# Linear attention in 128-token chunks with its normalisation on GpSimd, and a recurrence of 98 steps on 512 columns

## The reference

```python
def _L1_attn_ref(x, W, b):                 # x is the layer-normed t
    qkv = (x @ W.T + b).reshape(Bx, Tx, 3, Dx)
    q, k, v = (qkv[:, :, 0], qkv[:, :, 1], qkv[:, :, 2])
    q = jax.nn.elu(q) + 1.0
    k = jax.nn.elu(k) + 1.0
    kv = jnp.einsum('bti,btj->btij', k, v)
    kv_cum = jnp.cumsum(kv, axis=1)
    k_cum = jnp.cumsum(k, axis=1)
    num = jnp.einsum('bti,btij->btj', q, kv_cum)
    den = jnp.einsum('bti,bti->bt', q, k_cum)[..., None] + 1e-06
    return num / den
def _L1_ffn_ref(x, W, V, gamma, beta):     # x is the layer-normed t
    Wx = jnp.einsum('bti,hi->bth', x, W)
    ...                                    # batch norm over all tokens, gamma, beta
    def step(yt, wx_t):
        yt = jax.nn.sigmoid(wx_t + yt @ Vt)
        return (yt, yt)
...
t = t + _L1_attn_ref(_ln_t(t), L1_attn_W, L1_attn_b)
t = t + _L1_ffn_ref(_ln_t(t), L1_ffn_W, L1_ffn_V, L1_ffn_gamma, L1_ffn_beta)
```

## Time and profile before

| quantity | value |
|---|---|
| median of 3 runs | 2030.25 us (2029.51 to 2030.74) |
| profiled execution | 2031.14 us, of which the span of instructions is 2029.5 us |
| PE busy over the span | 1923.1 us (95%) |
| DVE / ACT / POOL busy | 1677.6 (83%) / 1465.6 (72%) / 1290.2 us (64%) |
| mean granted TensorE clock | 0.98 |

### The profile page before, as it was taken

The page is one execution under the profiler, slowest core; times in us unless marked ns, Lnnn a source line. Parts: engine busy times, 40 slices in busy tenths (PEclk is TensorE's granted clock), DMA queues, the critical chain, the costliest instruction groups (busy, mean ns, idle before and its releaser), DMA issues. The chain is left out here.

```text
span 2029.5 us, 64530 instructions
## 1 busy us (share of the span) xinstructions
PE 1923.1 (95%) x20434; PEld 1672.5 (82%) x20434; DVE 1677.6 (83%) x5427; ACT 1465.6 (72%) x3774; POOL 1290.2 (64%) x1760
## 2 busy tenths in 40 slices
PE   4999999999999997999999999999999995699997
PEld 2888888888888886899999999999999993466664
DVE  7888888888888885799999999999999992355554
ACT  3777777777777775799999999999999981122221
POOL 3888888888888885444544444444444445577772
PEclk9999999999999999899999999999999996899998
DMA  4343434443434322122222222222222212366663
GB/s 137 106 110 106 109 108 110 106 112 104 113 103 111 94 78 73 38 62 62 59 61 61 59 62 60 59 63 59 59 63 59 59 51 63 109 199 199 187 210 110
DMA packets 228620, 190.53 MB, mean 94 GB/s; under 512 B 19264, under 2 KB 187552, under 8 KB 228448
## 3 DMA queue, kind: packets, MB, share of 16 engines
q1 hardware_dynamic: 228448, 188.22, 33.3%
HBM read 111.08 MB, written 77.07 MB: 93 GB/s over the span
## 5 line engine op out<-in xcount | busy, mean ns | idle before, releaser
L830 POOL TENSOR_SCALAR la_spread<-la_mv 112x4 f32<-112x4 f32 x231 | 54.6, 236 | 388.5 <-DVE la_mv L916 388.1
L536 POOL TENSOR_TENSOR wa_prob<-wa_prob,wa_peak 128x784 f32<-128x784 f32 x128 | 194.5, 1520 | 118.4 <-DVE wa_peak L425 118.4
L788 ACT ACTIVATE la_raised<-k_psum,la_bqk 128x224 f32<-128x224 f32 x448 | 200.6, 448 | 73.9 <-PE k_psum L682 73.9
L838 POOL TENSOR_TENSOR la_ln<-la_spread,k_exponent 112x4 f32<-112x4 f32 x231 | 239.5, 1037 | 1.8 <-ACT la_u L771 0.3
L1274 ACT ACTIVATE main_y<-k_psum,sc_cols 128x448 f32<-128x448 f32 x112 | 70.9, 633 | 209.1 <-PE k_psum L1215 209.1
L682 PE MATMUL k_psum<-la_uT,la_wt 128*128 128x224 f32 x896 | 211.2, 358 | 0.0
L771 ACT ACTIVATE la_u<-la_xc,la_ln 112x128 f32<-112x128 f32 x448 | 201.1, 515 | 13.3 <-POOL la_ln L842 13.2
L805 ACT ACTIVATE la_u<-la_tn,la_ln 112x128 f32<-112x128 f32 x448 | 201.0, 515 | 10.2 <-POOL la_ln L842 10.2
L543 POOL TENSOR_TENSOR wa_prob<-wa_prob,wa_inv 128x784 f32<-128x784 f32 x128 | 194.8, 1522 | 10.1 <-DVE wa_inv L389 10.1
L789 ACT ACTIVATE la_positive<-k_psum,la_bqk 128x224 f32<-128x224 f32 x448 | 200.8, 448 | 0.0
L417 DVE TENSOR_TENSOR wa_prob<-k_psum,wa_bias 128x784 f32<-128x784 f32 x128 | 124.9, 976 | 83.1 <-PE k_psum L272 83.1
(11 more groups left out here) (147 smaller groups left out, 5879.2 us busy)
## 6 DMA issues: line engine op xcount, KB each, us to landing
wa_xw<-in_x_tok SPq DMA_DIRECT2D x128, 224.0 KB, 2.7
wa_xT<-in_x_cm SPq DMA_DIRECT2D x128, 196.0 KB, 2.5
la_xc<-x SPq DMA_DIRECT2D x224, 112.0 KB, 2.0
t<-la_tn SPq DMA_DIRECT2D x224, 112.0 KB, 2.0
main_tb<-t SPq DMA_DIRECT2D x28, 896.0 KB, 6.0
out<-main_ob SPq DMA_DIRECT2D x28, 896.0 KB, 7.6
x<-wa_y SPq DMA_DIRECT2D x128, 112.0 KB
x<-wa_y SPq DMA_DIRECT2D x128, 56.0 KB
```

The costliest lines, as they stand in the source:

```text
L536: nc.gpsimd.tensor_tensor(s, s, peak[:, k % S, :].unsqueeze(2).broadcast_to([128, PAIRS * HEADS, WIN]), ALU.subtract).then_inc(lowered, 1)
L788: nc.scalar.activation(raised[:, k, j, :], src, ACT.Exp, bias=bqk[:, j:j + 1])
L838: nc.gpsimd.tensor_tensor(rstd, spread[:, :], exponent[0:CH, 0:4], ALU.pow).then_inc(rooted, 1)
```

## The change

- Linear attention takes chunks of 128 tokens across image borders, 196 units of 256 tokens. A chunk that an image border cuts in half (`splits`) is masked and takes its outer product from its second half alone.
- The bias, and the mean over the weights that makes it cover the subtraction, are folded into the weights once (`fold`). The features of q and k come from one exp over 512 columns (ACT, `exps`, L793) and one max/min on DVE that reads PSUM (`combine`, L898).
- The running state is summed in PSUM: `outer(n, 0)` and `outer(n, 1)` each add one product, ACT copies the state out after each (`keep_state`, L817). DVE loses `advance`, `carry` and `values_out`.
- Both normalisations move from ACT to POOL, where each is a pair of tensor_scalar instructions on 128x128 (`normalise(n+2)`, L849, and `normalise2(n-5)`, L860). They stand behind `statistics(n+3)` in POOL's list.
- Everything is written out, no hardware loop is left.
- `scan` runs 98 steps on 512 columns (32 segments an image), in 14 batches of SB = 7; its input needs one POOL pass; the warm call has 2 batches of 6. The scale table goes out to memory and back before it.

```diff
             @block.gpsimd
             def _(pool):
                 pool.wait_ge(prep, 1)
-                def statistics(n, k):
+                def statistics(n):
...
                     pool.wait_ge(aggregated, n + 1)
-                    at_least(pool, shifted, n)
-                    apart(pool, passed)
-                    moments = mv[:, k].rearrange("p l a m -> p (l a) m")
-                    nc.gpsimd.tensor_scalar(spread[:, :], moments[:, :, 1], LN_EPS, None, ALU.add).then_inc(spread_out, 1)
-                    nc.gpsimd.tensor_scalar(minus[:, :], moments[:, :, 0], -1.0, None, ALU.mult).then_inc(minus_out, 1)
...
+                    nc.gpsimd.tensor_scalar(spread[:, :], mv[:, n % S].rearrange("p l a m -> p (l a) m")[:, :, 1], LN_EPS, None,
+                                            ALU.add).then_inc(spread_out, 1)
+                    pool.wait_ge(spread_out, n + 1)
+                    nc.gpsimd.tensor_tensor(rstd[:, n % S, :], spread[:, :], exponent[:, 0:4], ALU.pow).then_inc(rooted, 1)
...
+                def normalise(n):
+                    pool.wait_ge(rooted, n + 1)
+                    for a in range(2):
+                        last = nc.gpsimd.tensor_scalar(u[:, n % S, a, :], xc[:, n % XS, a, :], mv[:, n % S, 0, a, 0:1],
+                                                       rstd[:, n % S, a:a + 1], ALU.subtract, ALU.mult)
+                    last.then_inc(normed, 1)
...
-                def step(n, k):
-                    remember(n - AHEAD, k % S)
-                    statistics(n + 3, (k + 3) % S)
-                pipeline(pool, step, **run)
+                for n in steps:
+                    statistics(n + 3)
+                    normalise(n + 2)
+                    normalise2(n - 5)
...
-                def step(n, k):
-                    queries_and_keys(n, k % S)
-                    turn_keys(n - 1, (k - 1) % S)
-                    turn_tokens(n + 1, (k + 1) % S)
-                    numerators(n - 3, (k - 3) % S)
-                    moments(n - 8, k % S)
-                    outer(n - 2, (k - 2) % S)
-                    values(n + 1, (k + 1) % S)
-                    scores(n, k % S)
-                pipeline(pe, step, **run)
+                for n in steps:
+                    queries_and_keys(n)
+                    turn_keys(n - 1)
+                    turn_tokens(n + 1)
+                    outer(n - 2, 0)
+                    numerators(n - 3)
+                    moments(n - 8)
+                    outer(n - 2, 1)
+                    values(n + 1)
+                    scores(n)
...
+                for n in steps:
+                    measure(n + 3)
+                    denominators(n - 3)
+                    combine(n)
+                    invert(n - 3)
+                    aggregate(n + 3)
+                    attend(n - 3)
+                    inner_out(n)
...
+                for n in steps:
+                    exps(n)
+                    keys_out(n - 1)
+                    turned_out(n + 1)
+                    keep_state(n - 2, 0)
+                    values_out(n + 1)
+                    keep_state(n - 2, 1)
...
-        scan(nc, t2, out, 0, fT, vT, shift_bn, rstd, shift, start, final, ident, bank, "main")
+        scan(nc, t2, out, 0, 7, fT, vT, shift_bn, rstd, start, final, ident, bank, "main")
```

More of the change, by code:

```diff
@@ L620, in linear_attention, with rows, begins, splits @@
         k_turned, k_out = sem("la_k_turned"), sem("la_k_out")
-        kv_ready, moved, advanced = sem("la_kv_ready"), sem("la_moved"), sem("la_advanced")
+        kv_ready, kept = sem("la_kv_ready"), sem("la_kept")
         num_ready, den_ready, den_inv, attended = sem("la_num_ready"), sem("la_den_ready"), sem("la_den_inv"), sem("la_attended")
         normed2, counted, gram_done = sem("la_normed2"), sem("la_counted"), sem("la_gram_done")
[L625 to L631, removed]
+        def rows(dram, n):
+            return dram.rearrange("b t c -> (b t) c")[n * 2 * P:(n + 1) * 2 * P, :].rearrange("(a p) c -> p a c", p=P)
+        def begins(c):
+            return (c * P) % T == 0
+        def splits(c):
+            return (c * P) // T != (c * P + P - 1) // T
+        def ends(c):
+            return ((c + 1) * P) % T == 0
+        def outers(c):
+            return sum(not ends(i) for i in range(c))
+        steps = range(-4, UNITS + 9)
         with nc.Block() as block:
@@ L650, in store @@
+                def store(n):
+                    if not inside(n, UNITS):
                         return
                     sp.wait_ge(attended, n + 1)
-                    sp.dma_start(chunks(t2, n), tn[:, k]).then_inc(stored[k], 16)
-                def step(n, k):
-                    load(n + 4, (k + 4) % XS)
-                    store(n - 4, (k - 4) % XS)
-                pipeline(sp, step, **run)
+                    sp.dma_start(rows(t2, n), tn[:, n % XS]).then_inc(stored[n % XS], 16)
@@ L720, in outer @@
                         return
[L721 to L729 removed]
+                    if a == 0:
+                        pe.wait_ge(k_out, n + 1)
+                        pe.wait_ge(v_out, n + 1)
@@ new lines, in aggregate @@
+                def aggregate(n):
+                    if not inside(n, ROWS):
+                        return
+                    dve.wait_ge(measured, n + 1)
+                    at_least(dve, normed, min(UNITS, n - S + 1))
+                    at_least(dve, normed2, n - S - AHEAD + 1)
+                    for which, m in ((0, n), (1, n - AHEAD)):
+                        if inside(m, UNITS):
+                            for a in range(2):
+                                last = nc.vector.bn_aggr(mv[:, n % S, which, a, :], stats[:, n % S, which, a, :])
+                    last.then_inc(aggregated, 1)
@@ L1156, in _ @@
             def _(sp):
-                def step(j, k):
+                for j in range(-3, NB + 2):
                     if inside(j + 3, NB):
-                        kl = 1 - k
                         if out is not None:
@@ L1276, in _ @@
-                pipeline(act, step, **run)
+                for t in range(NT):
+                    act.wait_ge(v_done, t + 1)
+                    if out is not None:
+                        at_least(act, y_turned, t - 1)
+                    nc.scalar.activation(y[:, t % 2, :], b_state[t % 2][:, 0:COLS], ACT.Sigmoid, bias=shift_bn).then_inc(y_made, 1)
         if repeated:
```

585 lines of the change are left out of this document (267 added, 318 removed).

## The result

The changed kernel takes 2327.98 us (median of 4 runs, 2327.46 to 2329.79) against 2030.11 us (2029.51 to 2030.74) of the kernel before on the same chip. The ratio is 1.1469, with a 95% interval of 1.1449 to 1.1489: 14.7% slower. The forecast was slower by 220 us, to 2250, with a range up to 2313. The loss is 298 us, and the time lies outside the range.

What follows compares the result with a forecast made beforehand. A loop through PE, DVE and POOL was to bound linear attention at 5.49 us a unit instead of PE's 3.99. 221 - 2 + 0 + 1 = +220 us gave 2250 us, range 2190 to 2313.

Steps and rivals of the forecast that it cites:

- The loop: Linear attention: a chain through PE, DVE and POOL sets a 5.49 us period, PE idling 1.4 us before L682.
- Point 6 of the loop: POOL's pair of tensor_scalar on 128x128 takes 0.72 us, 0.38 an instruction; bounds 0.45 and 1.33.
- Points 4 and 5: On the loop: DVE to POOL 0.22 us; POOL's epsilon, power and two waits on its own results 1.62 us.
- Points 1, 2, 3 and 7: On the loop: PE's work 1.42 us; to combine 0.40; combine to aggregate 0.69, aggregates 0.36; POOL to PE 0.06.
- POOL's pair is dear: Rival, 4 in 100: POOL's normalisation pair at its upper bound, or slowed by DVE reading SBUF; period 6.10, time 2369 us.
- The clock: Rival, 3 in 100: PE's idling drops its granted clock; between 2250 and 2742 us, some 2500 if half the time.
- PE's work of 3.99 us: Linear attention: PE's work after the change sums to 3.99 us for a unit of 256 tokens.
- nothing else in a step is late: Linear attention: combine ends in time before scores, ACT's work and state copies fit, POOL's own load is 3.2 us.
- Ends of the stage: Linear attention's start about 1.5 us longer, its end about as much shorter: zero, within 3.
- The recurrence: The scan calls: main steps -6.4 us, warm call +3.0, main start +2.1, last store +3.5, prologue -1; together +1, within -5 and +9.

Runs made afterwards that it cites:

- Experiment 1: Changed kernel with one line moved in POOL's list, normalise(n+2) ahead of statistics(n+3): 2066.94 us, ratio 1.0183 to the kernel before.
- experiment 7: Changed kernel with only u's normalisation back on ACT, POOL computing a shift for it: 1986.18 us, ratio 0.9792 to the kernel before.
- experiment 2: Changed kernel, same order, POOL's four tensor_scalar a unit using multiply and add instead of subtract and multiply (values differ): 2188.49 us, ratio 1.0780.
- experiment 4: Changed kernel with an extra stage ahead timing tensor_scalar forms on POOL, alone and beside DVE: 2369.18 us (one run).
- experiment 6: Experiment 5 with combine(n) ahead of denominators(n-3) in DVE's list: 1956.55 us, ratio 0.9639 to the kernel before.
- experiment 3: Changed kernel with both edits, normalise(n+2) ahead of statistics(n+3) and multiply-add on POOL (values differ): 1980.82 us, ratio 0.9757.
- experiment 5: Changed kernel with normalise(n+2) ahead of statistics(n+3), the normalisation adding a mean negated by one small POOL instruction: 1981.33 us, ratio 0.9766.

## Why the prediction was wrong

The mechanism, its place and its direction were right; a term of its sum was mis-sized, the pair of tensor_scalar on the loop, and with it the time fell outside the range.

- **The loop.** Right, and shown. PE idles before L682, released by L849, 1.59 us a unit (308.6 / 194; 1.4 forecast). Experiment 1 opens the loop by order alone and gives 261 us back; experiment 7 opens it by taking the pair off POOL and gives 342.
- **Point 6 of the loop, the failed step.** It put the pair of tensor_scalar at 0.72 us; it measured 1.58, above its upper bound of 1.33 too. That bound was two rows of a form that multiplies and adds, and the pair subtracts. The step took the row of the same instruction name and the nearest size without asking whether its two operations were the same. Experiments 2 and 4 show that the operation is the cause of 353 of the 421 ns that an instruction took over the forecast (801 - 448). The other 68 are an error of the line itself: a fixed part of 342 ns where it had 240, made up in part by 0.83 ns a column where it had 1.13.
- **Points 4 and 5, too dear.** The way from DVE to POOL was 0.09, not 0.22. L837 to L841 was 0.36, not 0.41. And `normalise` follows the power after 1.03 us, where 1.04 + 0.17 had been added: it waits for `rooted` of the unit before, so there was no wait on POOL's own last result. That could be read in the order of POOL's list, and the prediction even says that the normalisation needs only older statistics; its sum did not use it. Together -0.36 us in this unit.
- **Points 1, 2, 3 and 7.** The first two 1.59 together plus 0.19, forecast 1.62 and 0.20; `combine` to aggregate 0.67 (0.69); aggregate 0.36 (0.36). Right within 0.03 each. Pair and way to PE 1.64, forecast 0.78. The whole: 5.49 + 0.86 - 0.42 = 5.93, the unit shown; the mean is 5.88. Point 6's error alone is 0.86 x 195 = 168 us; errors that cancelled hid half of it, and that was luck.
- **The rival "POOL's pair is dear"**, 4 in 100, is what happened, 0.8 us an instruction, though its time of 2369 was too high, for it kept the dear points 4 and 5. Its other suggested cause, DVE's reading of SBUF, is excluded by experiments 2 and 4 as more than the 8 ns between 793 and 801. The chance was too small for an operation that no row showed.
- **The clock.** The rival is false: the granted clock was 1.00 over 1165 us with PE 73% busy and an idle of 1.6 us in each period. The rows were the right guide. The Trainium skill, TensorE: Matmul & The Clock Gate, § A second HAM failure mode, tells of another kernel, in bf16 with 512 columns, in which short idles between groups of matmuls made the clock swing. Carried over to this kernel, as the prediction's rival did, that does not agree with this trace.
- **PE's work of 3.99 us** is right: 3.994 in experiment 6. But "nothing else in a step is late" was wrong by 0.12 us: with the loop open, `scores` waits for `combine` (experiments 3 and 6). It costs nothing at a period of 5.88, and 24.8 us at 4.1 (1981.33 - 1956.55).
- **Ends of the stage.** Forecast zero within 3, measured +6.9. The first `values` start at 817.7 instead of 813.6 (+4.1). POOL's first statistics start 2.2 us later (811.8 instead of 809.6), behind DVE's folding of the weights, which ends at 810.9. From there to the first `values` it is 5.9 us instead of 4.0, with two statistics and a pair of 1.59 ahead of them; in experiment 6 it is 4.0 again (812.7 to 816.7). At the other end, from the last `values` to the first DMA of the recurrence, it is 22.9 us instead of 20.1 (+2.8). Experiment 1, which mends the order and keeps the subtraction, has 22.8 there, and experiment 2, which does the reverse, 18.9. So POOL's dear instructions lengthen the end, not the loop.
- **The recurrence.** Forecast +1 within -5 and +9, measured -8.6, outside these bounds (338.1 us from its first DMA to the end of the span, against 346.7). Main steps are 2.581 apart, not 2.603 (-8.5 instead of -6.4). The start of the main call was forecast 2.1 later; from its first load to its first sigmoid it was 0.4 shorter, the load landing after 7 us where 9 were taken. The warm call was even, not +3. The end was +1.1, not +3.5; the prologue -0.95, as forecast. All but the prologue erred to the dear side.

In sum: 298.3 + 4.1 + 2.8 - 8.6 = 296.6 us of span, from 2029.5 to 2326.1, against 221 - 2 + 0 + 1 forecast. The period is where the forecast failed: 298 us against 219.

## What to carry to other kernels

When work moves to another engine's list, follow the lists round once: an instruction placed behind a wait that it does not need can close a loop through several engines, and then the sum round the loop is the period, with no engine full. Before rewriting anything, try the order of the lists; here one line moved in POOL's was worth 261 us and one in DVE's another 25. And take a price only from a row with the same operations and the same kind of operands; where there is none, widen the bounds beyond the nearest row, or measure the form by itself.

## What the runs showed that I had not expected

- On POOL a tensor_scalar of two operations costs 3.34 ns a column with a subtraction in it (subtract and multiply) and 0.83 without one (multiply and add): 793 against 448 ns on 128 columns, 1674 against 667 on 392. Adding the negated operand is the cheap form, and 4 columns for it are negated in one small instruction a unit. Why subtraction is dear no run tells.
- Two operations on column operands have a fixed part of some 340 to 370 ns (382 ns for 4 columns), where one operation on an immediate takes 234 (L837, 4 columns).
- A short wait of PE can be invisible as idle time: in experiments 3, 5 and 7 PE is busy 99.9% and still 3% slower than its work. It showed as a distance between starts of 0.55 instead of 0.46 us at one line.
